# Attention phases: the norm moved to the step before the projections, and the row maxima transposed, split and sent in two halves of the heads

## The chip, the cores and the metric

The kernel runs on one core of one Trainium2 chip. The metric is the device time of one execution in microseconds (us), the median of several executions. All durations below come from one profiled execution of the kernel before.

## What is computed

A four-layer transformer with adaptive layer norm over x of shape 16 x 256 x 128. Four of its parts are softmax attentions and are touched here; they carry the tile prefixes a0, a1, a2 and a4. For each batch row (256 tokens of 128 features) each of them computes

```python
h = _layernorm(x, axis=-1) * (1 + ca) + sa          # a4: RMS norm with a gain
q, k, v = project(h)                                # a4: rotary position on q and k
scores = jnp.einsum('bhqd,bhkd->bhqk', q, k) / scale
scores = jnp.where(jnp.asarray(causal), scores, -jnp.inf)   # a2: no mask
attn = jax.nn.softmax(scores, axis=-1)
out = jnp.einsum('bhqk,bhkd->bhqd', attn, v)
x = x + ga * (out @ w_out)
```

The head size is 8. a0, a2 and a4 have 16 query heads, a1 has 32 (pairs of them are subtracted from each other with a weight, and the result gets a root-mean-square norm of its own). The expert and feed-forward parts (f0 to f4), the linear attention and the norms between the parts are not touched.

## The kernel before

`attention_phase` runs one attention for all 16 batch rows. Its five engine programs walk through **steps** t = -2 to 16, and each step has one **slot** per head, 16 or 32 of them (`NH`). In step t the stages of different batch rows overlap: row t+2 is normed and projected, row t+1 gets its scores for the maxima, row t gets transposed scores, exponentials and the product with V, and row t-1 is finished. The slot at which an engine issues a piece is a constant (`L_QK`, `L_SPLIT`, `L_NMQ` and so on); each engine runs its pieces in the order of the slots and waits in that order, since an instruction never overtakes another one of its engine. `U` is 1 for 16 heads and 2 for 32.

The stages of one batch row, with the lines of the profile:

- **Norm.** L606 mean (matmul into bank 6), L755 XC, L481 square, L611 variance, L759 VE, L438 power -0.5 on POOL, L763/764 diagonal DG, L617 broadcast, L768 XN, L487 H. Slots 0 to 5 (times U).
- **Projections.** L628/629 (a4: L625/626) compute q and k from H into bank 6 at slot 6 (a4: q at 6, k at 8), DVE copies them to QKF one slot later, L634 computes v at slot 12 (22 for a1).
- **Split.** q and k are kept as three bf16 parts. L498 casts the high part (slot 8, in a4 slot 10), L448 on POOL takes the rest, L501 casts the middle part one slot later, L451 on POOL makes the low part. SP then issues 14 DMAs of 64 KB (a1: 26; L417/419), which lay the parts out by head in QH and KH, after two small ones that zero two rows (L413). The semaphore is `parts_sent`.
- **Scores for the maxima.** From slot 2 of the next step, two heads a slot (`score_slots`), L549 to L551 (a2: L554/555) write bank 0 or 1 and the reduce at L742 (a2: L745) takes their maxima. The first waits for `parts_sent`.
- **Maxima.** At slot 10 (`L_NMQ`, a1: 23), when all heads are reduced, L805/806 gather the maxima in NMQ, L688 transposes them into bank 7, L506 casts the high half (slot 11), L809 takes the low half, and ACT itself issues two small DMAs (L510, slot 12) that put both into rows of QH. The semaphore is `m_sent`.
- **Transposed scores.** In the next step, one head a slot, L567 to L569 (a2: L572/573), with the maxima already in the product; the first waits for `m_sent` of all heads. ACT exponentiates (L525), PE multiplies with V in bursts every fourth slot (L590), ACT copies a set (L471), PE turns it (L597, bank 7), DVE divides (L722, L728 or L733/735).
- **Output.** L670 transposes the context into bank 7 at slot 6, L519 copies it, L675 multiplies with the output weights, L829 (a4: L827) makes TMP at slot 8 and L832 adds it to x. In a1 there is a norm before it: L515, L815, a power on POOL (L455), L821.

Bank 7 is shared by the turns, the transposed maxima and the output, so each of them waits until the one before it has been read.

```python
L_MEAN, L_VAR, L_POW, L_DG, L_BC, L_XN, L_QK, L_V = 0, 2, 2, 3 * U, 4 * U, 5 * U, 6 * U, 10 * U + 2
L_SPLIT = [10] if rope else [L_QK + 2 + 2 * r * U for r in range(R)]
L_NMQ = L_SCORES + N_SCORES
...
after(pe, p_ready, b, p - 1)
if p == 0:
    after(pe, m_sent, b)
```

## Time and profile before

| | |
|---|---|
| median of 3 runs | 5114.13 us (5106.98 to 5117.71) |
| profiled execution, its own time | 5110.65 us |
| its span | 5108.9 us |
| mean granted TensorE clock | 0.804 of 2.4 GHz |
| TensorE matmul busy | 3976.6 us (78%) |
| VectorE busy | 2662.7 us (52%) |
| ScalarE busy | 1604.8 us (31%) |

Engines are PE (TensorE), DVE (VectorE), ACT (ScalarE), POOL (GpSimd) and SP (SyncE, which only issues DMAs here). In the rows a matmul reads `bank<-stationary,moving`. A row's bracket gives the idle time of its engine just before it and what ended that. The granted clock has two levels, 1.2 and 2.4 GHz, and a mean of 0.804 lies between them.

### The profile page before, as it was taken

The numbers are of one execution on the slowest core, as the hardware profiler recorded it, in microseconds if no ns is written. First come the engines' busy times: TensorE is split into PE (matmuls) and PEld (weight loads), VectorE is DVE, ScalarE is ACT, GpSimd is POOL, SyncE is SP. The second block draws the span as 40 slices with busy tenths as digits, with TensorE's granted clock in tenths as the row PEclk, the third lists the DMA queues.
The fourth block names the chain that finished last, engine by engine and source line by source line (L and its number), as shares of the span: only waits on it lengthen the run. The fifth ranks groups of instructions, "written<-read, shape, count | busy, mean of one in ns | idle before, by whom it ended". The sixth has DMA issues, their size and how long they took to land. (4 is left out here: it accounts for less than half of the span.)

```text
span 5108.9 us, 74218 instructions
## 1 busy us (share of the span) xinstructions
PE 3976.6 (78%) x20856; PEld 2273.6 (45%) x20936; DVE 2662.7 (52%) x5663; ACT 1604.8 (31%) x3308; POOL 592.7 (12%) x462
## 2 busy tenths in 40 slices
PE   4776679999957676767999789856666899546799
PEld 3454634444435454545444344434444545213544
DVE  4444655454466555644333355553333556896455
ACT  1434132222224444443333244423333322112321
POOL 1110100000012122210000011111111101442100
PEclk6878589999968888887999867776666798556699
DMA  3222100000032323220000000002222000000000
GB/s 57 32 28 26 50 9 1 1 0 0 4 42 29 38 28 40 28 51 3 1 1 0 6 19 18 18 13 26 25 26 37 3 0 0 2 0 5 20 1 16
DMA packets 150267, 89.53 MB, mean 18 GB/s; under 512 B 19049, under 2 KB 147315, under 8 KB 149235
## 3 DMA queue, kind: packets, MB, share of 16 engines
q1 hardware_dynamic: 143666, 81.61, 11.6%
q10 hardware_dynamic: 5760, 2.93, 0.3%
q0 software_dynamic: 576, 1.80, 0.2%
q8 instruction: 125, 2.05, 0.2%
q14 instruction: 140, 1.14, 0.1%
HBM read 26.35 MB, written 2.10 MB: 6 GB/s over the span
## 5 line engine op out<-in xcount | busy, mean ns | idle before, releaser
L525 ACT ACTIVATE a1PR<-bank 128x384 f32<-128x384 f32 x512 | 248.6, 492 | 302.2 <-PE bank L569 299.1
L1346 DVE TENSOR_TENSOR f1eHS<-f1eSG,bank 128x512 f32<-128x512 f32 x256 | 175.9, 687 | 319.8 <-PE bank L1274 229.8
L1341 DVE TENSOR_TENSOR f0eT<-f0eSG,bank 128x512 f32<-128x512 f32 x256 | 175.9, 687 | 312.7 <-PE bank L1255 293.2
L1305 ACT ACTIVATE f0eSG<-bank 128x512 f32<-128x512 f32 x256 | 152.8, 597 | 557.3 <-PE bank L1252 557.3
L1252 PE MATMUL bank<-f1NT,f1W 128*128 (+1 forms) x576 | 297.0, 597 | 15.0 <-DMA f1eSELB<-in_sel 14.8
L742 DVE TENSOR_REDUCE a1NM<-bank 128x3 f32<-128x384 f32 x512 | 266.1, 552 | 62.2 <-PE bank L551 56.2
L1274 PE MATMUL bank<-f1eHS,f1W 128*128 128x512 f32 x576 | 293.8, 592 | 1.2
L1252 PE MATMUL bank<-f0NT,f0W 128*128 (+1 forms) x512 | 262.5, 594 | 17.1 <-DMA f0eSELB<-in_sel 17.1
L1305 ACT ACTIVATE f1eSG<-bank,f1eFB 128x512 f32<-128x512 f32 x256 | 175.9, 687 | 283.6 <-PE bank L1252 152.8
L1274 PE MATMUL bank<-f0eHS,f0W 128*128 128x512 f32 x512 | 261.3, 592 | 1.6
L1255 PE MATMUL bank<-f0NT,f0W 128*128 (+1 forms) x512 | 262.3, 594 | 0.0
L742 DVE TENSOR_REDUCE a4NM<-bank 128x3 f32<-128x384 f32 x256 | 130.2, 550 | 164.6 <-PE bank L551 164.0
L525 ACT ACTIVATE a4PR<-bank 128x384 f32<-128x384 f32 x256 | 121.6, 489 | 267.7 <-PE bank L569 266.8
L1346 DVE TENSOR_TENSOR f0eHS<-f0eT,bank 128x512 f32<-128x512 f32 x256 | 175.9, 687 | 54.6 <-PE bank L1274 49.7
L745 DVE TENSOR_REDUCE a2NMQ<-bank 128x2 f32<-128x512 f32 x256 | 162.6, 682 | 68.4 <-PE bank L555 66.8
L525 ACT ACTIVATE a2PR<-bank 128x512 f32<-128x512 f32 x256 | 146.5, 594 | 140.2 <-PE bank L573 140.0
L549 PE MATMUL bank<-a1KH,a1QH 128*128 128x128 bf16 x512 | 126.5, 249 | 71.4 <-DVE a1NM L742 65.7
L525 ACT ACTIVATE a0PR<-bank 128x384 f32<-128x384 f32 x256 | 121.1, 490 | 191.2 <-PE bank L569 171.3
L1252 PEld LDWEIGHTS bank<-f1NT,f1W 128*128 128x128 f32 x576 | 109.3, 191 | 155.9 <-issue 154.3
L567 PE MATMUL bank<-a1QH,a1KH 128*128 128x128 bf16 x512 | 122.0, 241 | 70.8 <-DMA a1QH<-a1M 63.6
L742 DVE TENSOR_REDUCE a0NM<-bank 128x3 f32<-128x384 f32 x256 | 130.1, 551 | 85.8 <-PE bank L551 84.8
L1274 PEld LDWEIGHTS bank<-f1eHS,f1W 128*128 128x128 f32 x576 | 109.4, 190 | 130.1 <-issue 120.0
(597 smaller groups left out, 9286.8 us busy)
## 6 DMA issues: line engine op xcount, KB each, us to landing
a1QH<-a1SPL SPq DMA_DIRECT2D x192, 64.0 KB
a1KH<-a1SPL SPq DMA_DIRECT2D x192, 64.0 KB
a0QH<-a0SPL SPq DMA_DIRECT2D x96, 64.0 KB
a0KH<-a0SPL SPq DMA_DIRECT2D x96, 64.0 KB
f0W<-in_w SPq DMA_DIRECT2D x3, 2048.0 KB, 13.4
a2QH<-a2SPL SPq DMA_DIRECT2D x96, 64.0 KB
a4QH<-a4SPL SPq DMA_DIRECT2D x96, 64.0 KB
a4KH<-a4SPL SPq DMA_DIRECT2D x96, 64.0 KB
```

What stands on the lines that cost most here:

```text
L525: nc.scalar.activation(PR[:, h % 8, :], bank[2 + h % 2][:, 0:NC], ACT.Exp, scale=SCALE)\
L549: pe.matmul(o[:, 0:P], q(0), k(0), start=True, stop=True)
L567: pe.matmul(o[:, 0:P], k(0), q(0), start=True, stop=True)
L742: v.tensor_reduce(NM3[:, h, :], bank[h % 2][:, 0:NC].rearrange("p (n k) -> p n k", n=3), AX, ALU.max, negate=True).then_inc(s_used.sem, 1)
L745: v.tensor_reduce(NMQ[:, :, h], bank[h % 2][:, 0:NC].rearrange("p (n k) -> p n k", n=2), AX, ALU.max, negate=True).then_inc(s_used.sem, 1)
L1252: pe.matmul(bank[q][:, :], W1[:, m * P:(m + 1) * P], x, start=True, stop=True).then_inc(g_ready.sem, 1)
L1255: pe.matmul(bank[2 + q][:, :], W3[:, m * P:(m + 1) * P], x, start=True, stop=True).then_inc(u_ready.sem, 1)
L1274: mm = pe.matmul(bank[6 + j][:, :], W2[:, m, :], HS[:, m % 4, :], start=(m == 0), stop=(m == NCH - 1 and CBF is None))
L1305: nc.scalar.activation(dst, bank[q][:, :], fn, bias=FB[:, m:m + 1] if cfg.get("hbias") else 0.0)\
L1341: v.tensor_tensor(T1[:, :], a, bank[2 + q][:, :], ALU.mult).then_inc(t1_ready.sem, 1)
L1346: v.tensor_tensor(HS[:, m % 4, :], a, bank[4 + (j * NBC + kth[m]) % 2][:, :], ALU.mult).then_inc(hs_ready.sem, 1)
```

## The change

In every attention phase the norm of a batch row runs one step earlier than its projections (stage t+3, with H in three buffers), so the steps begin at t = -3, and the slots are dealt out anew. Projections come at slot 0 (a1: 0 and 4; a4: 0 and 2), the high cast at slot 2 (a1: 2 and 6; a4: 5), the middle cast two slots after it, v at slot 2 (a1: 8; a4: 4), and the norm takes the slots behind v. The maxima go in two halves of the heads, each with a transpose, a cast, a subtraction and two DMAs of its own, at slots 7 and 10 (a1: 13 and 24), on semaphores `m_sent_0` and `m_sent_1`; the transposed scores wait for the second half at head NH/2. The turns come one slot earlier, and with them the output.

The diff, cut to its core (U, R, QK as above; HG is NH/2):

```diff
         SPL = sb("SPL", [P, R, 3, 2, T], BF16)
         NM3 = sb("NM3", [P, NH, 3])
...
+        M2 = sb("M2", [HG, 2, 2, T], BF16)
         ZR = sb("ZR", [NH, T], BF16)
...
-                for k in range(2, 5):
+                for k in range(1, 4):
                     step(i * 3 + k, k % 3)
-            for t in range(14, 17):
+            for t in range(13, 17):
                 step(t, t % 3)
...
-        L_MEAN, L_VAR, L_POW, L_DG, L_BC, L_XN, L_QK, L_V = 0, 2, 2, 3 * U, 4 * U, 5 * U, 6 * U, 10 * U + 2
-        L_SPLIT = [10] if rope else [L_QK + 2 + 2 * r * U for r in range(R)]
+        L_QK = [2 * n * U for n in range(QK)]
+        L_V = 2 * QK * U if not rope else 4
+        L_SPLIT = [5] if rope else [L_QK[r] + 2 for r in range(R)]
+        L_MEAN = L_V + 2
+        L_SQ = L_MEAN + 2 if centered else L_MEAN
+        L_VAR = L_SQ + U
+        L_VE = L_VAR + 1
+        L_DG = L_VE + U
+        L_BC = L_DG + 1
+        L_XN = L_BC + 1
+        L_H = L_XN + 1
         L_SCORES = 2
         N_SCORES = cfg["score_slots"]
         heads_at = lambda h: range(*(min(max(k - L_SCORES, 0), N_SCORES) * NH // N_SCORES for k in (h, h + 1)))
-        L_NMQ = L_SCORES + N_SCORES
-        L_MT = L_NMQ
-        L_MSPLIT = L_MT + 1
-        L_MSEND = L_MSPLIT + 1
+
+        L_NMQ = [13, 24] if diff else [7, L_SCORES + N_SCORES]
         burst_at = lambda h: ((h - 5) // 4 % NU, 0 if h >= 5 else -1) if h % 4 == 1 else None
         copy_at = {(4 * PK * (s + 1) + 2) % NH: (s, (4 * PK * (s + 1) + 2) // NH) for s in range(NS)}
-        turn_at = {4 * PK * (s + 1) + 4: s for s in range(NS)}
+        turn_at = {4 * PK * (s + 1) + 3: s for s in range(NS)}
...
+        turned_at = {p + 1: s for p, s in turn_at.items()}
         late = lambda h, at: [(s, p // NH) for p, s in at.items() if p % NH == h]
-        L_LAST = 4 * PK * NS + 4 - NH
+        turns_before = lambda h: sum(p < h for p in turn_at)
+        L_LAST = 4 * PK * NS + 3 - NH
         L_COMBINE = L_LAST + 2
         L_CTT = L_COMBINE + 4 if diff else L_LAST + 2
         L_OUT, L_TMP = L_CTT + 1, L_CTT + (1 if diff else 2)
...
-                        b = t + 2
-                        if h == L_POW:
+                    if has(3, t):
+                        b = t + 3
+                        if h == L_VE:
                             after(pool, ve_ready, b)
                             after(pool, dg_ready, b - 1)
                             nc.gpsimd.tensor_tensor(RS[:, :], VE[:, :], c.HALF[:, 0:2], ALU.pow).then_inc(rs_ready.sem, 1)
+                    if has(2, t):
...
-                        if h == L_MEAN:
+                    if has(3, t):
+                        b = t + 3
+                        if h == L_SQ:
...
-                        if h == L_XN:
+                        if h == L_H:
                             after(act, xn_ready, b)
-                            after(act, v_ready, b - 1)
+                            after(act, v_ready, b - 3)
                             scale, shift = (c.MOD[:, l, 1, one(b)], c.MOD[:, l, 0, one(b)]) if centered else (COL[:, 3:4], 0.0)
-                            nc.scalar.activation(H[:, :], XN[:, :], ACT.Identity, bias=shift, scale=scale).then_inc(h_ready.sem, 1)
+                            nc.scalar.activation(H[:, m, :], XN[:, :], ACT.Identity, bias=shift, scale=scale).then_inc(h_ready.sem, 1)
+                    if has(2, t):
+                        b = t + 2
...
@@ -496,18 +511,20 @@
                                 after(act, f_ready, b, None if rope else r + 1)
                                 after(act, parts_sent[r], b - 1)
                                 nc.scalar.copy(SPL[:, r, 0, :, :], QKF[:, :, :]).then_inc(hi_ready.sem, 1)
-                            if h == L_SPLIT[r] + 1:
+                            if h == L_SPLIT[r] + 2:
                                 after(act, res_ready, b, r + 1)
                                 nc.scalar.copy(SPL[:, r, 1, :, :], RES[:, :, :]).then_inc(mid_ready.sem, 1)
-                    if has(1, t) and h == L_MSPLIT:
+                    for g in range(2 if has(1, t) else 0):
                         b = t + 1
-                        after(act, mt_ready, b)
-                        after(act, m_sent, b - 1)
-                        nc.scalar.copy(M2[:, 0, :], bank[7][0:NH, 0:T]).then_inc(mhi_ready.sem, 1)
-                    if has(1, t) and h == L_MSEND:
-                        after(act, mlo_ready, t + 1)
-                        for a in range(2):
-                            act.dma_start(QH[MAX0 + a:MAX0 + a + 1, (m + 1) % 3, :, :], M2[:, a, :]).then_inc(m_sent.sem, 16)
+                        if h == L_NMQ[g] + 1:
+                            after(act, mt_ready, b, g + 1)
+                            after(act, m_sent[g], b - 1)
+                            nc.scalar.copy(M2[:, g, 0, :], bank[7][0:HG, 0:T]).then_inc(mhi_ready.sem, 1)
+                        if h == L_NMQ[g] + 2:
+                            after(act, mlo_ready, b, g + 1)
+                            for a in range(2):
+                                act.dma_start(QH[MAX0 + a:MAX0 + a + 1, (m + 1) % 3, g * HG:(g + 1) * HG, :], M2[:, g, a, :])\
+                                    .then_inc(m_sent[g].sem, 16)
                     if has(-1, t):
                         b = t - 1
                         if diff and h == L_COMBINE:
...
 
             def scores_t(b, j, p):
                 after(pe, p_ready, b, p - 1)
-                if p == 0:
...
             def step(t, m):
                 for h in range(NH):
                     if has(2, t):
-                        b = t + 2
+                        b, j = t + 2, (m + 2) % 3
...
+                                if rope:
+                                    w = (WQ, WK)[n]
+                                    pe.matmul(bank[6][:, 0:T], w[:, 0:P], H[:, j, :], start=True, stop=True)
+                                    mm = pe.matmul(bank[6][:, T:2 * T], w[:, P:2 * P], H[:, j, :], start=True, stop=True)
+                                else:
+                                    pe.matmul(bank[6][:, 0:T], WQ[:, n * P:(n + 1) * P], H[:, j, :], start=True, stop=True)
+                                    mm = pe.matmul(bank[6][0:KR, T:2 * T], WK[:, n * P:n * P + KR], H[:, j, :], start=True, stop=True)
+                                mm.then_inc(qk_ready.sem, 1)
+                        if h == L_V:
+                            after(pe, qk_copied, b)
+                            for n in range(2):
+                                mm = pe.matmul(bank[6][:, n * SV * VW:(n + 1) * SV * VW], H[:, j, n * P:(n + 1) * P], WV[:, :],
+                                               start=True, stop=True)
+                            mm.then_inc(v_ready.sem, 1)
+                    if has(3, t):
+                        b = t + 3
                         if h == L_MEAN and centered:
                             after(pe, v_copied, b - 1)
...
@@ -645,15 +664,12 @@
                     for s, back in late(h, turn_at):
                         if has(-back, t):
                             b = t - back
-                            if s == 0 and not diff:
+                            after(pe, cx_ready, b, s)
+                            if turns_before(L_OUT) == s and not back:
                                 after(pe, tmp_ready, b - 1)
-                            else:
-                                after(pe, cx_ready, b, s)
-                            if s == (1 if diff else 0):
-                                after(pe, tmp_ready, b - 1)
-                            if 4 * PK * (s + 1) + 4 - 4 * PK < L_MT < 4 * PK * (s + 1) + 4 and has(1 - back, t):
-                                after(pe, mhi_ready, b + 1)
-                                after(pe, mlo_ready, b + 1)
+                            for g in range(2):
+                                if turns_before(L_NMQ[g]) == s and not back and has(1, t):
+                                    after(pe, mlo_ready, t + 1, g + 1)
                             turn(b, s)
                     if has(-1, t):
                         b = t - 1
...
                             mm.then_inc(o_ready.sem, 1)
-                    if has(1, t) and h == L_MT:
+                    for g in range(2 if has(1, t) else 0):
                         b = t + 1
-                        if causal:
-                            after(pe, nmq_ready, b)
-                        else:
-                            after(pe, s_used, b)
-                        if diff and has(0, t):
-                            after(pe, cx_ready, t, (L_MT - 8) // 4 + 1)
-                        if has(-1, t):
-                            after(pe, tmp_ready, t - 1)
-                        for n in range(2):
-                            mm = pe.transpose(bank[7][0:NH, n * P:(n + 1) * P], NMQ[:, n, :], c.ID)
-                        mm.then_inc(mt_ready.sem, 1)
+                        if h == L_NMQ[g]:
+                            if causal:
+                                after(pe, nmq_ready, b, 2 * g + 2)
+                            else:
+                                after(pe, s_used, b, HG * (g + 1))
+                            if has(0, t):
+                                after(pe, cx_ready, t, turns_before(L_NMQ[g]))
+                            if has(-1, t):
+                                after(pe, tmp_ready, t - 1)
+                            if g:
...
                             maxima(b, n)
-                        if h == L_NMQ and causal:
-                            after(v, s_used, b)
-                            v.tensor_copy(NMQ[:, 0, :], NM3[:, :, 0]).then_inc(nmq_ready.sem, 1)
-                            v.tensor_tensor(NMQ[:, 1, :], NM3[:, :, 1], NM3[:, :, 2], ALU.min).then_inc(nmq_ready.sem, 1)
-                        if h == L_MSPLIT:
-                            after(v, mhi_ready, b)
-                            v.tensor_tensor(M2[:, 1, :], bank[7][0:NH, 0:T], M2[:, 0, :], ALU.subtract).then_inc(mlo_ready.sem, 1)
+                        for g in range(2):
+                            heads = slice(g * HG, (g + 1) * HG)
+                            if h == L_NMQ[g] and causal:
+                                after(v, s_used, b, HG * (g + 1))
+                                after(v, mt_ready, b - 1, g + 1)
+                                v.tensor_copy(NMQ[:, 0, heads], NM3[:, heads, 0]).then_inc(nmq_ready.sem, 1)
+                                v.tensor_tensor(NMQ[:, 1, heads], NM3[:, heads, 1], NM3[:, heads, 2], ALU.min).then_inc(nmq_ready.sem, 1)
+                            if h == L_NMQ[g] + 1:
+                                after(v, mhi_ready, b, g + 1)
+                                v.tensor_tensor(M2[:, g, 1, :], bank[7][0:HG, 0:T], M2[:, g, 0, :], ALU.subtract).then_inc(mlo_ready.sem, 1)
```

In `maxima`, and for the turns on DVE, only waits are changed to fit; the operations are the same.

The order on ACT in a4, in the loop over steps, of before. a4SPL<-a4QKF is the high cast, a4SPL<-a4RES the middle cast, a4M the halves of the maxima, a4CTS a set's copy, a4PR an exponential:

```order
L498 CAST a4SPL<-a4QKF 128x512 [waits parts_sent]
...
L525 ACTIVATE a4PR<-bank 128x384 [waits st_ready]
...
L471 COPY a4CTS<-bank 128x256 [waits t_ready]
...
L501 CAST a4SPL<-a4RES 128x512 [waits res_ready]
...
L506 CAST a4M<-bank 16x256 [waits m_sent]
...
L510 DMA a4QH<-a4M 1x16x256 [waits mlo_ready]
```

The same engine and phase after the change, from the high cast to the first pair of DMAs (a4CTT is the copy ahead of the output product):

```order
L513 CAST a4SPL<-a4QKF 128x512 [waits parts_sent]
...
L536 ACTIVATE a4CTT<-bank 128x256 [waits o_ready]
L236 ISA
L542 ACTIVATE a4PR<-bank 128x384 [waits st_ready]
...
L516 CAST a4SPL<-a4RES 128x512 [waits res_ready]
...
L522 CAST a4M<-bank 8x256 [waits m_sent_0]
...
L526 DMA a4QH<-a4M 1x8x256 [waits mlo_ready]
...
L522 CAST a4M<-bank 8x256 [waits m_sent_1]
...
L526 DMA a4QH<-a4M 1x8x256 [waits mlo_ready]
```

The two casts of the split stood between the exponentials just ahead of the maxima's cast; now they stand well ahead of both halves, and there are two casts of maxima and four DMAs where there were one and two.

The order on PE in a4 after the change, at slot 7, where the first half of the maxima is transposed (L707) between the last transposed scores of slot 7 (L584 to L586) and the next scores for maxima (L566); before, no transpose stood among the scores for maxima:

```order
L584 MATMUL bank<-a4QH,a4KH 128x128 [waits p_ready]
L585 MATMUL bank<-a4QH,a4KH 128x128
L586 MATMUL bank<-a4QH,a4KH 128x128
L236 ISA
L236 ISA [waits nmq_ready]
L236 ISA [waits cx_ready]
L707 MATMUL bank<-CST,a4NMQ 8x128 [waits tmp_ready]
L707 MATMUL bank<-CST,a4NMQ 8x128
L236 ISA
L566 MATMUL bank<-a4KH,a4QH 128x128 [waits s_used]
```

The transpose waits for the gathered maxima of half the heads and for TMP of the row before, and the scores behind it wait with it.

## Rows read from the trace of the kernel before

**Rows 1.** Windows of eleven steps in a0, a1, a2, a4: stretch, length, busy us, PEclk.
```profile
143.34:443.95 300.61, 213.45 (x2068) 148.60 (x2068) 136.05 (x352) 118.52 (x276) 33.05 (x33) 0.80 0.29 30
1573.58:2146.03 572.45, 395.91 (x4048) 284.63 (x4048) 327.88 (x891) 244.51 (x550) 118.16 (x66) 0.83 0.30 34
3004.77:3285.71 280.94, 254.37 (x1726) 132.52 (x1728) 157.48 (x341) 132.45 (x264) 35.25 (x33) 0.76 0.08 18
3511.18:3875.06 363.88, 228.37 (x2090) 162.75 (x2090) 137.61 (x363) 116.81 (x276) 49.06 (x55) 0.67 0.25 25
```
**Rows 2.** Waits in a4's window: us in total, times, longest.
```profile
PE bank L549 <- DMA a4QH<-a4SPL: 68.1, 11, 7.7
PE bank L567 <- DMA a4QH<-a4M: 23.5, 11, 2.5
PE bank L597 <- DVE a4M L809: 19.5, 11, 1.9
ACT a4SPL L498 <- POOL a4QKF L442: 17.0, 11, 1.5
PE bank L688 <- DVE a4NMQ L806: 15.8, 11, 1.4
```
**Rows 3.** Waits in a0's window.
```profile
PE bank L567 <- DMA a0QH<-a0M: 36.6, 11, 4.3
PE bank L549 <- DMA a0QH<-a0SPL: 18.9, 11, 3.1
```
**Rows 4.** Waits in a1's window.
```profile
PE bank L567 <- DMA a1QH<-a1M: 42.0, 9, 6.8
PE bank L670 <- DVE a1CX L733: 40.8, 11, 3.7
```
**Rows 5.** Waits in a2's window.
```profile
PEld bank L572 <- DMA a2QH<-a2M: 4.0, 7, 1.0
PE bank L554 <- DMA a2QH<-a2SPL: 3.3, 3, 1.2
```
**Rows 6.** Timeline of a4: start us, us, engine line op out<-in, [idle before <-releaser].
```profile
3638.05 1.21 SPq L413 DMA_DIRECT2D a4QH<-a4ZR  x2
...
3640.74 1.17 ACTq L510 DMA_DIRECT2D a4QH<-a4M  x2
...
3646.04 0.29 PE L567 MATMUL bank<-a4QH,a4KH 128*128 128x128 bf16 x1 [2.30 <-DMA a4QH<-a4M]
...
3646.79 1.51 PE L590 MATMUL bank<-a4PR,a4VX 128*32 128x256 f32 x16
...
3655.13 0.29 PE L549 MATMUL bank<-a4KH,a4QH 128*128 128x128 bf16 x1 [5.89 <-DMA a4QH<-a4SPL]
```
**Rows 7.** Timeline of a0 around the maxima of one step.
```profile
326.36 0.54 DVE L829 TENSOR_SCALAR a0TMP<-bank,a0COL,MOD 128x256 f32<-128x256 f32 x1
...
326.95 0.86 PE L590 MATMUL bank<-a0PR,a0VX 128*32 128x256 f32 x16
...
327.53 1.01 DVE L742 TENSOR_REDUCE a0NM<-bank 128x3 f32<-128x384 f32 x2
...
328.98 0.38 PE L688 MATMUL bank<-CST,a0NMQ 128*16 128x128 f32 x2 [0.89 <-DVE a0NMQ L806]
...
329.88 0.41 DVE L809 TENSOR_TENSOR a0M<-bank,a0M 16x256 bf16<-16x256 f32 x1 [1.04 <-ACT a0M L506]
...
330.33 1.39 ACTq L510 DMA_DIRECT2D a0QH<-a0M  x2
...
338.24 0.29 PE L567 MATMUL bank<-a0QH,a0KH 128*128 128x128 bf16 x1 [4.17 <-DMA a0QH<-a0M]
```
**Rows 8.** Timeline of a1: the value projection, and the power on POOL.
```profile
1771.09 1.13 PE L634 MATMUL bank<-a1WV,a1H 128*128 128x256 f32 x4
...
1797.03 5.43 POOL L455 TENSOR_TENSOR a1CR<-a1CM,HALF 128x32 f32<-128x32 f32 x1 [5.92 <-DVE a1CM L817]
```

More of the change, by code:

```diff
@@ L738, in maxima @@
                 after(v, s_ready, b, h + 1)
-                if h == 0:
+                if h == 0 and not causal:
                     after(v, mt_ready, b - 1)
@@ L832, in step @@
                             v.tensor_tensor(DST[:, tok(b)], DST[:, tok(b)], TMP[:, :], ALU.add).then_inc(x_updated.sem, 1)
[L833 removed]
+                    for s, back in late(h, turned_at):
                         if has(-back, t):
                             turned(t - back, (m - back) % 3, s)
[L836 to L837 removed]
+                if isinstance(t, int) and t < -1:
+                    fill(t + 4)
             steps(v, step)
```

101 lines of the change are left out of this document (45 added, 56 removed).

## The prediction

> **What bounds the kernel now.** I read the granted clock first: it is 0.804 on average, so part of the matmul time is run at 1.2 GHz. Then the busy time by stretches, to find the touched phases, and in each a window of eleven steps, cut from one square of the norm to the eleventh after it [rows 1]. The columns there are the stretch, its length, then the busy time of PE, PE's weight loads, DVE, ACT and POOL, then the granted clock. Divided by 11, one step takes 27.3 us in a0, 52.0 in a1, 25.5 in a2 and 33.1 in a4. PE is busy 19.4, 36.0, 23.1 and 20.8 us of them, at a clock of 0.80, 0.83, 0.76 and 0.67. DVE has 12.4, 29.8, 14.3 and 12.5 us of work, ACT 10.8, 22.2, 12.0 and 10.6. So no engine but PE in a2 is near its limit. a0 and a4 do nearly the same arithmetic, and a4 takes 5.8 us more: there a wait must stand.
>
> Next the waits in the four windows. In a4 [rows 2] PE waits for the parts of q and k (a4SPL) 68.1/11 = 6.2 us a step and for the maxima (a4M) 23.5/11 = 2.1. In a0 [rows 3] it is 1.7 and 3.3, in a1 [rows 4] 42.0/11 = 3.8 for the maxima, in a2 [rows 5] 0.3 and 0.4. These are waits of the engine that all the others follow, so they lie on the path.
>
> The timeline shows why. In a4 SP issues its first DMA behind the high cast at 3638.05 and the scores that need the last of them start at 3655.13 [rows 6]: 17.1 us from cast to landing. The two small DMAs of the maxima are issued at 3640.74, and the first transposed scores start at 3646.04, 5.3 us later; in a0 it is 330.33 to 338.24, 7.9 us [rows 7]. After the high cast a4 has six slots left in the step and two in the next, which are worth 17.1 less the two waits of 6.2 and 2.1, some 9 us; after the issue of the maxima every phase with 16 heads has four slots left. Both are less than the landing takes.
>
> **What the change does to each wait.** The high cast moves from slot 8 to slot 2 in a0, from 10 to 5 in a4, so its DMAs have 16 and 13 slots before the scores need them. If a step is some 22 us long, the cast in a4 comes about 6 us into it (estimate: 22/16 us a slot, less a little, since the first slots have no scores) and lands at 6 + 0.6 + 17.1 = 24; the scores at slot 2 want it at 22 + 3 = 25 (same estimate). So the parts' wait goes, in a4 with about 1 us to spare. The first half of the maxima goes out at slot 9 instead of 12, some 10 to 11 us into the step, plus 5.3 to 7.9 for landing: 16 to 19, ahead of the next step at 22. The second half still goes at slot 12, but is wanted only at head 8. In a1 the halves have 17 and 22 slots. That wait goes everywhere.
>
> Per step, waits removed: a0 1.7 + 3.3 = 5.0, a1 3.8, a2 0.7, a4 6.2 + 2.1 = 8.3.
>
> **The clock.** After the wait in a4 a burst with V takes 1.51 us for 16 matmuls [rows 6], in a0 at the upper level 0.86 [rows 7], so a wait costs again in what follows it. At full clock PE's busy time would shrink by 19.4 x 0.20 = 3.9 us in a0, 36.0 x 0.17 = 6.1 in a1, 20.8 x 0.33 = 6.9 in a4, and 23.1 x 0.24 = 5.5 in a2. From both sides: nothing of it is a gain (the clock stays as it is), or most of it. The nearest row is a2: it hardly waits for a DMA, and is at 0.76. So full clock is not what follows when those waits are gone. I take a quarter: 1.0, 1.5 and 1.7 us, and nothing in a2.
> The Trainium skill (TensorE: Matmul & The Clock Gate, "Loop structure matters more than you think") says that a DMA wait between groups of matmuls drops the clock and that matmuls kept back to back hold it. By that rule alone the whole reduction would be had, which is the first rival; the rows of a4 agree with the first half of it, the clock of a2 speaks against the second.
>
> **Other gains.** In a4 the casts of the split stand right ahead of the maxima's cast in ACT's order, and the high cast waits 17.0/11 = 1.5 us for POOL. PE then waits 1.4 us for the gathered maxima (L688) and 1.8 us at the turn for their low half (L597) [rows 2]. The new order has both casts out of the way; in a0, where they always were, L688 waits 0.89 [rows 7]. I take 1.8 of the 3.2 us. In a1 PE waits 40.8/11 = 3.7 us for the context [rows 4], behind a power of 5.43 us on POOL [rows 8]. The power stays, but the projection of v, 1.13 us [rows 8], now stands at slot 8 in front of that wait instead of at slot 22: 0.6 us gained. POOL now has part of the split around the power, and ACT's middle cast of the second half may have to wait for it at slot 8; that is in the 1.1 below.
>
> **New costs.** A second pair of transposes (0.38 us), a second cast and subtraction (0.41), and a second pair of DMAs on ACT's queue, which holds ACT for 1.39 us [rows 7]. ACT's share and the subtraction lie in the slots in which DVE sets the pace with its two reduces of 1.01 us together, and ACT has half its time free: nothing, while DVE stays slower there. The norm's pieces on DVE leave those slots in about the same number as new ones enter. What counts is the place on PE: at slot 7 the first transposes wait for the gathered maxima and for TMP (0.54 us [rows 7]), and the scores behind them wait too, so DVE runs dry for some 0.3 us (estimate: transposes 0.38 plus the first scores, less the addition to x that DVE still has). The turn now follows the second half's transposes after one slot instead of two; between them lies the chain of 1.04 us wait and 0.41 us subtraction: 0.2 more. Sum 0.9 us a step in a0 and a4. In a2, where PE is busy 91% of the time, I put 1.2, in a1 1.1. Bounds of this cost: 0 (all of it beside DVE's reduces) and 5.6 (last rival).
> The Trainium skill (DMA: Bandwidth & Descriptors, "Rules for kernel authors") speaks against this part: small transfers should be coalesced, since under 64 KB one pays mostly overhead. The halves are 4 KB each. The rows show that overhead as 1.39 us of ACT's queue a pair; if all of it were exposed, the sum would be worse by 1.39 x 64 = 89 us.
>
> The added step t = -3 holds one norm, which stood at the start of step -2 before: nothing.
>
> **The sum**, per batch row: a0 -5.0 - 1.0 + 0.9 = -5.1; a1 -3.8 - 1.5 - 0.6 + 1.1 = -4.8; a2 -0.7 + 1.2 = +0.5; a4 -8.3 - 1.7 - 1.8 + 0.9 = -10.9. Together -20.3, times 16 batch rows = -325 us. The profiled execution took 5110.65 us, so 4786; the median of the runs is 3.5 us above it, so **4789 us**.
>
> **Rivals.**
> 1. *The clock stays up too.* Half of the shrinking in a0, a1 and a4 and 4 us in a2, where PE is nearly the limit: 1.0 + 1.5 + 1.7 + 4.0 = 8.2 us a row beyond my sum, 131 us: 4658. For it: the low stretches follow waits in a0 and a4. Against: a2. Chance 0.13.
> 2. *Only the waits go, and new ones take part of it.* No clock gain, none of the 1.8 and 0.6, and twice the new costs: a0 -3.2, a1 -1.6, a2 +1.7, a4 -6.5, together -9.6 x 16 = -154: 4960. For it: PE, DVE and ACT are in lockstep in every slot. Chance 0.13.
> 3. *The DMAs become the floor of a4.* The step there can't be shorter than 17.1 + 0.6 plus the way from slot 2 to slot 5, three pairs of reduces and the rope work, 3 to 4 us: 21 to 22. If the four small DMAs in the same traffic stretch the landing by 2 us, the step is 24 instead of 22.2: +29 us, 4818. Chance 0.12.
> 4. *Slower: PE's order.* The transposes now stand among the scores, and nothing overtakes them. Each first half could stop PE for two reduces, TMP, transposes and subtraction (1.01 + 0.54 + 0.38 + 0.41 = 2.3), each second for the gathering and the chain to the turn (0.89 + 1.04 = 1.9), and ACT's issue be exposed (1.39): 5.6 us in each of 64 steps, 358 us against 285 us of removed waits (17.8 x 16): +73, 5187. It decides from 4.5 us a step on. Against: in before the same chain costs PE about 1 us a step in a0. Chance 0.04.
> 5. *No effect:* another engine holds the step at its length. DVE's 12.4 of 27.3 us speaks against it, and the order shows that casts and sends do move. Chance 0.03.
>
> **How the numbers follow.** The forecast has 0.55. The range 4690 to 4920 holds it with its bounds, rival 3 and part of rivals 1 and 2; outside lie about half of each of these two, the slower case and no effect. A measurement of this kernel tells 0.2%, 10 us, from no change. Faster by more: 0.55 + 0.13 + 0.13 + 0.12 = 0.93; within: 0.03; slower: 0.04.
>
> **What would show it.** In the changed profile the step of a4 should be 21 to 24 us, a0 21 to 23, a1 46 to 49, a2 25 to 27. PE's waits for the maxima should be near 0 in all phases and for the parts near 0 in a0, under 1 us in a4. New waits should show at the first half's transposes, ended by DVE, of 1 to 2 us on PE. I am wrong if a4's wait for parts is still over 2 us, if a2 loses over 2 us a step, or if the transposes' waits sum to over 4 us a step.

## The result, and the profile after

The changed kernel takes **4894.3 us** (median of 4, 4886.36 to 4904.15) against 5115.92 (4 runs, 5106.98 to 5130.74) of the kernel before: ratio 0.9565, 95% interval 0.9535 to 0.9595. The forecast was 4789 in a range of 4690 to 4920: the direction and the range held, but only two thirds of the expected gain came. The number lies nearer to rival 2 (4960, new waits eat part of the gain) than to the forecast.

| | before | after |
|---|---|---|
| span of the profiled execution, us | 5108.9 | 4902.4 |
| mean granted clock | 0.804 | 0.827 |
| TensorE matmul busy, us | 3976.6 | 3986.4 |
| a0, first memset to last TMP, us | 484.7 | 403.5 |
| a1 | 880.4 | 885.0 |
| a2 | 452.1 | 459.7 |
| a4 | 563.2 | 416.6 |

The four phases sum to -215.6 us; the rest of the kernel, which the change does not touch, took 9 us more in this profile. The windows of after that answer to [rows 1], again from one square of the norm to the eleventh after it (stretch, length, busy time of PE, its weight loads, DVE, ACT, POOL, then clock), in the order a0, a1, a2, a4:

```profile
120.21:365.29 245.08, 202.36 (x2091) 139.88 (x2091) 142.68 (x386) 118.76 (x287) 33.07 (x33) 0.85 0.35 37
1473.28:2040.45 567.17, 416.12 (x4070) 286.24 (x4070) 339.47 (x925) 245.13 (x562) 117.80 (x66) 0.81 0.32 34
2910.33:3191.43 281.10, 234.63 (x1739) 125.26 (x1738) 163.09 (x354) 134.45 (x276) 33.05 (x33) 0.84 0.07 17
3415.78:3666.27 250.49, 204.27 (x2113) 139.21 (x2113) 144.68 (x397) 116.58 (x288) 49.18 (x55) 0.89 0.35 36
```

Divided by 11, a step and its split into PE busy and PE idle:

| phase | before: step = busy + idle | after | predicted step |
|---|---|---|---|
| a0 | 27.3 = 19.4 + 7.9 | 22.3 = 18.4 + 3.9 | 22.2 |
| a1 | 52.0 = 36.0 + 16.0 | 51.6 = 37.8 + 13.7 | 47.2 |
| a2 | 25.5 = 23.1 + 2.4 | 25.6 = 21.3 + 4.2 | 26.0 |
| a4 | 33.1 = 20.8 + 12.3 | 22.8 = 18.6 + 4.2 | 22.2 |

The step is as forecast within 0.6 us in three phases; a1 alone is off, by 4.4, and outside the 46 to 49 us that the prediction named for it. Now the waits of PE in the same windows. In a4, where [rows 2] had 68.1 and 23.5 us of DMA waits:

```profile
PE bank L707 <- DVE a4TMP L851: 15.5, 11, 1.4
PE bank L614 <- DVE a4M L833: 11.2, 11, 1.2
...
PE bank L584 <- DMA a4QH<-a4M: 3.6, 4, 2.6
```

The wait for the parts is gone, that for the maxima is 0.3 us a step. The new wait stands at the first half's transposes (L707), 1.4 us a step and ended by DVE, where the prediction looked for it. a0 has the same pair (15.1 and 11.3 us) and no DMA wait. In a1 the 42.0 us of [rows 4] for the maxima are gone too, but:

```profile
PE bank L566 <- DVE a1NM L761: 45.8, 89, 1.0
PE bank L686 <- DVE a1CX L752: 40.4, 11, 4.6
PE bank L614 <- ACT a1CTS L484: 30.1, 33, 2.2
PE bank L707 <- DVE a1CX L752: 10.9, 11, 1.1
PE bank L630 <- issue: 10.4, 3, 3.5
```

and ACT stands once a step at the middle cast of a1's second half, because POOL does its 5.43 us power first. This is the timeline of one such place (start, duration, engine and line, idle time before it and what ended that):

```profile
1770.09 5.43 POOL L468 TENSOR_TENSOR a1CR<-a1CM,HALF 128x32 f32<-128x32 f32 x1 [3.21 <-DVE a1CM L841]
...
1775.48 1.15 POOL L461 TENSOR_TENSOR a1RES<-a1QKF,a1SPL 128x512 f32<-128x512 f32 x1
1775.55 1.63 DVE L845 TENSOR_TENSOR a1CX<-a1CX,a1CR 128x512 f32<-128x512 f32 x1 [2.55 <-POOL a1CR L468]
1776.66 0.62 ACT L516 CAST a1SPL<-a1RES 128x512 bf16<-128x512 f32 x1 [5.05 <-POOL a1RES L461]
```

Two suspects come from this: ACT blocked for 5.05 us, and DVE's scaling of the context, which starts with POOL's subtraction and takes 1.63 us.

The end of a phase gained nothing either. These are the two steps in which the phase a2 runs empty, first of before, then of after; they do the same attention work, in nearly the same number of matmuls (142 and 108, then 140 and 117):

```profile
3302.90:3325.10 22.20, 19.65 (x142) 9.89 (x142) 12.35 (x25) 10.90 (x22) 1.45 (x2) 0.77 0.09 21
3325.10:3338.60 13.50, 11.21 (x108) 5.04 (x108) 3.70 (x10) 9.02 (x19) 0.00 (x0) 1.00 0.01 2
```
```profile
3221.40:3249.40 28.00, 25.21 (x140) 11.74 (x140) 12.80 (x26) 10.72 (x22) 0.00 (x0) 0.54 0.00 1
3249.40:3271.90 22.50, 19.74 (x117) 8.55 (x118) 5.28 (x13) 9.73 (x20) 0.00 (x0) 0.54 0.01 2
```

At 0.54 PE is busy for 19.7 us in the second of them, and was for 11.2 at full clock.

### The profile page after: what moved, and what is told of

Same layout as the page of the kernel before. It is cut to its first block and busy times, and to the rows that moved or that the text cites. A ratio compares the mean times of both kernels' runs of the same rounds, so it can differ in the third digit from the quotient of the medians.

```text
span 4902.4 us, 75514 instructions
## 1 busy us (share of the span) xinstructions
PE 3986.4 (81%) x21064; PEld 2255.4 (46%) x21064; DVE 2695.0 (55%) x5823; ACT 1612.1 (33%) x3372; POOL 584.9 (12%) x462
## 3 DMA queue, kind: packets, MB, share of 16 engines
q1 hardware_dynamic: 143666, 81.61, 12.2%
## 5 line engine op out<-in xcount | busy, mean ns | idle before, releaser
L1370 DVE TENSOR_TENSOR f0eHS<-f0eT,bank 128x512 f32<-128x512 f32 x256 | 176.0, 688 | 54.6 <-PE bank L1298 49.6
L566 PE MATMUL bank<-a1KH,a1QH 128*128 128x128 bf16 x512 | 127.0, 248 | 74.6 <-DVE a1NM L761 66.4
L1276 PEld LDWEIGHTS bank<-f0NT,f0W 128*128 128x128 f32 x512 | 97.7, 191 | 139.6 <-issue 139.2
## 6 DMA issues: line engine op xcount, KB each, us to landing
f0W<-in_w SPq DMA_DIRECT2D x3, 2048.0 KB, 12.2
```

The source lines that it names most:

```text
L566: pe.matmul(o[:, 0:P], q(0), k(0), start=True, stop=True)
L1276: pe.matmul(bank[q][:, :], W1[:, m * P:(m + 1) * P], x, start=True, stop=True).then_inc(g_ready.sem, 1)
L1370: v.tensor_tensor(HS[:, m % 4, :], a, bank[4 + (j * NBC + kth[m]) % 2][:, :], ALU.mult).then_inc(hs_ready.sem, 1)
```

## The experiments

The table gives what all comparisons below rest on: the window from the fourth to the fifteenth square of each phase, divided by 11, as PE busy + PE idle at the mean granted clock. It is one profiled execution each; the ratios are against the kernel before in the same session. How far a step can be read shows where kernels have the same code in a phase: after, e1, e2 and e5b agree within 0.6 us in a0 and 0.2 in a4, e10 and e13 within 0.1 in a1, but in a2 e9b, e10 and e13 have 24.7, 24.7 and 22.5. A difference of 2 us in a2 shows nothing by itself.

| kernel | us, ratio | a0 | a1 | a2 | a4 |
|---|---|---|---|---|---|
| before | 5115.9 | 19.4+7.9 .80 | 35.9+16.0 .83 | 23.7+2.3 .74 | 20.6+12.2 .68 |
| after | 4894.3, .9565 | 18.1+3.9 .87 | 37.8+13.7 .81 | 21.9+4.0 .82 | 18.5+4.2 .90 |
| e1 | 4816.9, .9398 | 17.7+4.1 .89 | 33.2+13.2 .92 | 21.7+4.0 .83 | 18.5+4.4 .90 |
| e2 | 4806.6, .9388 | 17.7+4.0 .90 | 34.2+11.7 .87 | 21.9+4.0 .81 | 18.4+4.4 .90 |
| e3 | 4920.5, .9589 | 18.0+4.0 .87 | 38.4+13.4 .77 | 23.0+3.6 .77 | 19.5+6.0 .85 |
| e4 | 5195.6, 1.0128 | 20.3+8.1 .76 | 36.6+12.9 .83 | 25.0+4.3 .71 | 20.5+13.3 .73 |
| e5b | 4864.2, .949 | 17.4+4.1 .91 | 37.3+13.0 .82 | 22.9+3.7 .78 | 19.0+3.7 .86 |
| e6b | 4860.1, .9458 | 17.6+4.0 .89 | 35.5+11.1 .84 | 23.2+3.6 .76 | 19.9+6.0 .83 |
| e8b | 5183.3, 1.0111 | 21.0+7.6 .74 | 35.8+14.7 .84 | 25.6+4.0 .68 | 20.0+11.3 .74 |
| e9b | 4790.7, .9316 | 16.2+3.5 .97 | 34.6+11.7 .85 | 22.6+2.0 .76 | 18.4+7.1 .87 |
| e12 | 4875.5, .9512 | 16.9+4.0 .93 | 34.9+12.7 .86 | 28.4+1.8 .57 | 19.2+4.5 .84 |
| e10 | 4712.9, .922 | 15.9+3.2 .98 | 33.6+10.4 .87 | 22.7+2.1 .76 | 18.6+5.0 .87 |
| e13 | 4683.3, .9192 | 16.1+3.2 .97 | 33.3+10.5 .88 | 20.1+2.5 .88 | 19.0+3.7 .86 |
| e14 | 4838.2, .9433 | 16.5+3.2 .95 | 39.4+13.6 .75 | 21.6+2.4 .83 | 19.0+3.9 .86 |

**e1: the second projection of a1 moved away from the power.**

```diff
-        L_QK = [2 * n * U for n in range(QK)]
-        L_V = 2 * QK * U if not rope else 4
+        L_QK = [0, 8] if diff else [2 * n * U for n in range(QK)]
+        L_V = 12 if diff else 2 * QK * U if not rope else 4
```

> Only in a1: the second projection goes from slot 4 to 8, its split from slot 6 to 10, v from 8 to 12, and the norm follows. The power on POOL then stands ahead of the second split in time. Theory A (POOL's order: the second split waits behind the power of 5.4 us, ACT's middle cast waits 4.9 us for it, and POOL's subtraction next to DVE's scaling of the context stretches that): both waits go, a step of a1 falls from 51.6 to about 47.5 us, the kernel by some 60 us to 4835. Theory B (the turns, one slot earlier, cost it: PE waits 2.7 us a step for ACT's copies): nothing changes, 4894.

Measured 4816.93 us (4812.91 to 4818.9), 77 under the changed kernel, and a1's step is 46.4 instead of 51.5. ACT's wait for POOL fell from 54.6 to 0.7 us in eleven steps. Theory A's number holds, with a little more than it gave, so the loss does hang on the slots that a1's second half was given. But the two windows say how: idle time is nearly equal (13.7 and 13.2 us a step), PE busy is not (after first, then e1):

```profile
1424.50:1990.50 566.00, 415.82 (x4070) 286.09 (x4068) 338.82 (x924) 245.10 (x563) 117.79 (x66) 0.81 0.33 35
```
```profile
1419.60:1930.10 510.50, 364.82 (x4072) 255.03 (x4070) 324.70 (x926) 240.70 (x563) 118.38 (x66) 0.92 0.35 38
```

The same 4070 matmuls take 51 us less, at 0.92 instead of 0.81. Of 5.0 us a step, 4.6 are the clock.

**e2: e1, and a1's turns and what follows them back in their old slots.**

```diff
-        turn_at = {4 * PK * (s + 1) + 3: s for s in range(NS)}
+        turn_at = {4 * PK * (s + 1) + (4 if diff else 3): s for s in range(NS)}
-        L_LAST = 4 * PK * NS + 3 - NH
+        L_LAST = 4 * PK * NS + (4 if diff else 3) - NH
```

(and a1's second maxima at slot 23 instead of 24.)

> The same as the first kernel, and in a1 also the turns one slot later, as they were before the change, with the second half of the maxima at slot 23. Theory A: within 10 us of the first kernel. Theory B: PE's waits for ACT's copies fall from 2.7 to under 1 us a step, a1 gains 1.7 to 2.7 us a step, 25 to 40 us in all.

4806.55 us (4803.01 to 4818.29): 10 us under e1, less than the two spreads can tell apart, as theory A has it. In the profile a1 has 1.5 us a step less idle time and 1.0 more busy time.

**e3: maxima in one piece, the rest of the change kept.** `L_NMQ` is `[24]` in a1 and `[10]` elsewhere, one transpose, cast, subtraction and pair of DMAs for all heads.

> The changed kernel with the maxima in one piece again (slot 10, in a1 24), the norm ahead kept: half of the change alone. If the halves are what removes the waits for the maxima, these come back (3.3, 3.8, 0.4 and 2.1 us a step in a0, a1, a2, a4, together 9.6) and the halves' own cost goes (about 1 us in each): 5.6 x 15 = 84 us more than the changed kernel, 4978. If the earlier split alone clears the DMA traffic for them, they stay near 0 and it is about 60 us faster than the changed kernel, 4835.

4920.52 us (4899.98 to 4933.78): the median is 26 us over the changed kernel's, 12% of its gain, in between the two theories. The intervals of the two ratios overlap, but the profiles put the difference in a4, where the step is 25.4 instead of 22.7. What the halves were for, the wait for the maxima, is gone in a0 without them. The DMA issues show why. In a0 ACT sends the maxima long after SP's last part and well before its next one:

```profile
271.77 0.61 SPq L429 DMA_DIRECT2D a0QH<-a0SPL  x1
...
279.29 1.15 ACTq L527 DMA_DIRECT2D a0QH<-a0M  x2
...
285.89 1.21 SPq L425 DMA_DIRECT2D a0QH<-a0ZR  x2
```

In before, the maxima of a0 were issued in the middle of SP's twelve parts, and their reader started 7.9 us later [rows 7]. (The DMAs of 64 KB are twelve a batch row, and 24 in a1; the 14 and 26 named with the stages include the two small ones.) In a4 of e3 they still go out right behind the parts in some steps, and 2.7 us behind them in others:

```profile
3523.44 0.61 SPq L429 DMA_DIRECT2D a4QH<-a4SPL  x1
...
3524.41 1.15 ACTq L527 DMA_DIRECT2D a4QH<-a4M  x2
...
3532.63 0.29 PE L585 MATMUL bank<-a4QH,a4KH 128*128 128x128 bf16 x1 [4.57 <-DMA a4QH<-a4M]
...
3550.15 0.61 SPq L429 DMA_DIRECT2D a4QH<-a4SPL  x1
...
3552.83 1.15 ACTq L527 DMA_DIRECT2D a4QH<-a4M  x2
...
3559.26 0.23 PE L585 MATMUL bank<-a4QH,a4KH 128*128 128x128 bf16 x1 [1.62 <-DMA a4QH<-a4M]
```

From issue to the first reader it is 8.2 us in the first case and 6.4 in the second, and PE's wait falls from 4.57 to 1.62. Over a whole phase the median from issue to landing of the maxima's DMAs is 3.2 us in before and 1.9 in e3 for a0, 4.2 and 2.1 for a1. So moving the norm ahead also takes the parts' traffic out of the way of the maxima.

**e4: halves and earlier turns alone, with norm, projections and casts in their old slots and step.**

```diff
+        L_QK = [6 * U + 2 * n * U for n in range(QK)]
+        L_V = 10 * U + 2
+        L_SPLIT = [10] if rope else [L_QK[r] + 2 for r in range(R)]
+        L_MEAN, L_SQ, L_VAR, L_VE, L_DG, L_BC, L_XN, L_H = 0, 0, 2, 2, 3 * U, 4 * U, 5 * U, 5 * U
```

> The maxima in two halves and the turns one slot earlier as in the changed kernel, but norm, projections and casts in the slots and the step where they were before: the other half of the change alone. If the two parts each remove their own wait: the parts' wait stays (1.7 us in a0, 6.2 in a4), the maxima's goes, 9.6 - 4 = 5.6 us a row, 84 us less than before, 5030. If the halves only pass the wait on to the parts: a4 gains nothing and the kernel is within 20 us of 5115 less what a0 and a1 give, some 5070.

5195.57 us (5177.36 to 5208.45), 1.3% slower than before (interval 0.9% to 1.7%), where both theories had it faster. No wait for the maxima is left, in any phase, and yet a4's step is 33.8 instead of 32.8. PE's waits in a4 are now (compare [rows 2]):

```profile
PE bank L559 <- DMA a4QH<-a4SPL: 78.9, 11, 8.3
PE bank L607 <- DVE a4M L826: 26.1, 11, 2.4
PE bank L700 <- DVE a4TMP L844: 17.1, 11, 1.6
PE bank L700 <- DVE a4NMQ L823: 11.5, 11, 1.2
```

The two DMA waits of before, 68.1 + 23.5 = 91.6 us, have become one of 78.9: the wait for the maxima stood just ahead of the wait for the parts, and what it gives back is mostly waited for two slots later. The rest went to the turns (L607, 19.5 before) and to TMP (L700). In a0 it is 36.6 + 18.9 = 55.5 before [rows 3] and 45.6 in e4.

**e5b: after, with a1's second middle cast at slot 11 and no other change.** This takes ACT's wait away and leaves POOL's order and its overlap with DVE.

```diff
-                            if h == L_SPLIT[r] + 2:
+                            if h == L_SPLIT[r] + (5 if diff and r else 2):
```

> The changed kernel with one number different: in the two-softmax phase (a1) the middle cast of the second half stands at slot 11 instead of 8. GpSimd still does the normalization's power (5.43 us) ahead of its share of that split, beside VectorE. Theory A1 (the cost was ScalarE standing in order behind a cast whose input was late, 4.9 us a step): the 54 us of wait of ScalarE in eleven steps go, a1's step falls from 51.5 to about 46.5 us as in e1, and the time comes to 4815 to 4850 us. Rival A2 (the cost is VectorE and GpSimd stretching each other in that stretch, whatever ScalarE does): the step stays at 50 or more, 4880 to 4900 us.

4864.22 us (4857.83 to 4890.06), between both. ACT's wait went from 54.6 to 0.6 us, and a1's step from 51.5 only to 50.3: theory A1 falls as an account of the 5 us, since it gives 1.1. A2 fits this step, and DVE's scaling, 1629 ns in after (and 1628 in e5b), takes 693 ns in e1, which seems to speak for it:

```profile
L845 DVE TENSOR_TENSOR a1CX<-a1CX,a1CR x11: 1629/1629/1631, 1463.5 to 1981.1; 128x512 f32<-128x512 f32 x11
```
```profile
L845 DVE TENSOR_TENSOR a1CX<-a1CX,a1CR x11: 693/693/694, 1452.0 to 1915.4; 128x512 f32<-128x512 f32 x11
```

But it is 1629 ns again in e2, whose a1 step is 45.9 us, beside 46.4 in e1, and in e13, the fastest kernel of all, with 43.8 us. So A2 falls too: the stretch by 0.94 us is real and costs little.

**e6b: e1 with one piece everywhere.**

> e1 with the maxima in one piece in all four phases. Theory (halves pay only where the maxima's transfer is still waited for, which e3's trace has as 2.6 us a step in a4 and nothing elsewhere): a4's step 25.4 instead of 22.9, thirteen times, so 4816.9 + 20 to 40 = 4837 to 4857 us. Rival 1 (with a1's step 5 us shorter, its transfer of the maxima is waited for again, up to the 3.8 us a step that it cost before the change): another 50, about 4900. Rival 2 (no piece matters, e3's difference was the clock): 4815 to 4820.

4860.09 us (4845.21 to 4870.17), 43 over e1, just above the end of what the theory gave and far from rival 1. a4 is 25.9 (+3.0 us), a2 26.9 (+1.2), a1 46.6 (+0.1): in a1 no wait for the maxima came back. The halves pay in a4; the 1.2 us of a2 are within what equal code differs by there.

**e8b: before with the turns one slot earlier, nothing else.** e4's slots with `NP = 1`, so one piece; a1's maxima come at slot 24 instead of 23.

> The kernel before with one thing of the change alone: the transposes of the context stand one slot earlier, and what follows them with them; maxima in one piece, normalization in its old place. e4 (this and the halves) measured 1.4 % over before. Theory T (the cost is in the earlier transposes, which wait for VectorE's update of X to leave their bank, 1.7 us a step in e4's a0 and a2): nearly all of e4's loss shows here, 5170 to 5200 us. Theory H (the cost is in the second set of casts, transposes and sends): 5110 to 5135 us, as before.

5183.26 us (5169.42 to 5204.26), ratio 1.0111 (1.0069 to 1.0154): most of e4's loss, theory T by the number. The wait that T named, for the update of X, is not there. In a0 PE waits for DVE's reduces instead, a wait that before's list for these steps does not have:

```profile
PE bank L560 <- DVE a0NM L755: 24.8, 25, 1.6
```

In a0 and a2 the step rises by 1.3 and 3.6 us, and PE's busy time by 1.6 and 1.9 at a lower clock (.80 to .74 and .74 to .68); a1 and a4 are 1.4 and 1.5 us shorter, which does not make up for it.

**e9b: the norm ahead alone.** e3 with the turns back: one piece, turns in their old slots (`turn_at` + 4, `L_LAST` with them, a1's maxima at slot 23).

> The changed kernel with the normalization one step ahead and nothing else: maxima in one piece, the transposes of the context in their old slots (e3 had them one slot earlier, 4920.5 us). Theory T (the earlier transposes cost 1.5 to 3 us a step wherever they stand): 50 to 100 us under e3, 4820 to 4870. Theory H or none: 4910 to 4925, as e3. e1 and e2 differ by the turns of a1 alone and are equal within 10 us, which speaks for the latter at least in a1.

4790.68 us (4762.93 to 4806.57), 130 us under e3 and 104 under the full change; more than theory T had given. a0 of e3, then of e9b:

```profile
95.30:336.90 241.60, 197.71 (x2088) 135.25 (x2081) 138.68 (x353) 114.91 (x277) 33.07 (x33) 0.87 0.36 38
```
```profile
96.90:313.50 216.60, 178.12 (x2072) 122.20 (x2068) 135.27 (x349) 116.86 (x276) 33.04 (x33) 0.97 0.42 42
```

and two of PE's waits there, e3 and e9b:

```profile
PE bank L567 <- DVE a0NM L762: 21.9, 41, 1.5
PE bank L615 <- DVE a0M L834: 11.6, 11, 1.2
```
```profile
PE bank L615 <- DVE a0M L834: 8.0, 11, 0.8
...
PE bank L567 <- DVE a0NM L762: 4.8, 20, 0.3
```

With the turn one slot earlier PE waits 21.9 instead of 4.8 us in eleven steps for DVE's reduces of the scores (as I read it, DVE has the turned context to scale just then). Idle time changed by about 0.5 us a step in sum, the busy time by 1.8 at .87 and .97: the greater part is again the clock. The ends of the phases went back too: the two steps in which a2 runs empty are 25.0 and 13.5 us here, where after has 28.0 and 22.5.

**e12: the full change with the turns back**, halves transposed at slots 8 and 10 (13 and 23 in a1).

> The changed kernel with the transposes of the context (and what follows them) back in their old slots; normalization ahead and halves stay, their sends at slots 8 and 10 (13 and 23 in a1). With e3 and e9 (one piece, turns early and back: 4920.5 and 4790.7) and the changed kernel (4894.3) this fills a square of four. Theory T (the early turns cost about 2.3 us a step in a0, 5.4 in a1, 1.9 in a2, half of it and more as a lower clock of TensorE): steps of 19.7, 46.3 and 24.7 as in e9, and in a4, where e9 still waits 4.3 us a step for the maxima, 21 to 23; 4740 to 4790 us. Rival H (the halves' second set of casts and sends crowds the slots just as the early turns do): 4800 to 4880.

4875.52 us, but with a spread that needs a look: 4879.98, 4873.87, 4877.18 and 4814.17, with clocks of .815, .816, .817 and .833. The median lies in the range of rival H, but H's reason, crowded slots, covers little of it: over e9b a0 and a1 have 1.2 and 1.3 us a step more, and a4 has 1.9 less. Against the changed kernel a0 and a1 came down, to 20.9 and 47.6 us a step from 22.0 and 51.5. Of the 87 us by which the four phases of e12 are over those of e9b in the profiles, 84 are a2, which went up to 30.1 with hardly any wait left:

```profile
2802.70:3134.30 331.60, 312.10 (x1742) 162.37 (x1738) 162.97 (x349) 135.24 (x276) 33.00 (x33) 0.57 0.06 16
```

In a1, e9b and e12 show where the loss came from. With the turns in their old slots POOL's power stands at slot 6, behind the second split, and with the early turns at slot 5, ahead of it. This is POOL in e12, where after has the power first:

```profile
1721.22 1.15 POOL L461 TENSOR_TENSOR a1RES<-a1QKF,a1SPL 128x512 f32<-128x512 f32 x1 [1.24 <-ACT a1SPL L513]
...
1725.85 5.42 POOL L468 TENSOR_TENSOR a1CR<-a1CM,HALF 128x32 f32<-128x32 f32 x1
```

In the eleven steps ACT does not wait for POOL at its casts in either kernel, and the steps are 46.3 and 47.6 us, near the 46.4 of e1, which parts the two the other way. So the early turns and the second projection at slot 4 cost together: taking back either gives 3.9 to 5.4 us a step, and once the projection is at slot 8 the early turns cost 0.5 (e2 to e1).

**e10 and e13: the parts that pay.** Norm ahead, turns back, one piece in a0, a1, a2, halves in a4 alone, and e1's later projection in a1. e13 also gives a4 the early turns of the change, and its first half slot 7 instead of 8:

```diff
+    NP = 2 if cfg.get("plain") else 1
-        turn_at = {4 * PK * (s + 1) + 3: s for s in range(NS)}
+        turn_at = {4 * PK * (s + 1) + 5 - NP: s for s in range(NS)}
```

> Normalization ahead, turns in the old slots, one piece in a0, a1 and a2, halves in a4 alone, and a1's second projection at slot 8 as in e1. From e9: a4's step falls by up to the 4.3 us that it waits for the maxima, 35 to 50 in all; a1's step is already 46.3 there, as in e1, with no wait of ScalarE for GpSimd, so theory A (that wait was a1's whole trouble) expects nothing more: 4740 to 4760 us. Rival (the later projection brings its own 5 us a step): 4670 to 4700.

> As e10, but in a4 the turns one slot earlier with the halves, as in the changed kernel. Theory T (early turns cost wherever they stand): a4's step 1 to 2 us above e10's, 15 to 25 us in all. Rival (in a4 they pay with the halves, as the change has it): equal or 10 us below e10.

e10 4712.94 us (4692.4 to 4740.74), below theory A's 4740 and above the rival's 4700: the later projection brings 2.4 us a step in a1 (46.3 to 43.9) and not 5. e13 **4683.32 us** (4675.13 to 4724.35), ratio 0.9192 (0.9136 to 0.9249): 8.1% under before and 211 us under the change. In a4 the early turns and the earlier first half together are 0.8 us a step better, against theory T, and no wait for the maxima is left there (12.4 us in eleven steps of e10). The two intervals overlap, and the larger part of the difference between the profiles is a2 (24.7 and 22.5 us a step), where the two kernels have the same code.

**e14: e13 with the turns of a0, a1 and a2 one slot later still.**

> e13 with the turns of a0, a1 and a2, and all behind them, one slot later again (9, 17 of the next step and so on, where the kernel before has 8 and 16); a4 stays as in e13. Theory T continued (each slot gives VectorE time to have the maxima and the scaled context ready before TensorE comes to the turn; in e9 TensorE still waits 4.8 us in eleven steps for the maxima in a0 and 10.0 in a2, and 46.7 in a1 for the scaled context): steps shorter by 0.2 in a0, up to 0.5 in a2 and up to 4 in a1, 4620 to 4670 us. Rival (the old slots were the right ones: what the later turn frees at its start it takes at the end, where the output's matmuls and the halves or maxima share the bank): 4690 to 4740 us.

4838.17 us (4819.19 to 4854.58, 6 runs): 155 over e13, worse than the rival's 4740. Most of it is in a1 (53.0 us a step against 43.8), e13 first:

```profile
1385.60:1867.40 481.80, 366.41 (x4051) 260.69 (x4050) 320.35 (x892) 239.16 (x552) 117.74 (x66) 0.88 0.35 40
```
```profile
1393.10:1976.20 583.10, 433.78 (x4048) 301.95 (x4048) 326.21 (x892) 244.38 (x550) 117.66 (x66) 0.75 0.31 34
```

3.1 us a step of new waits came with 6.1 us a step of busy time at a lower clock. The old slots were the right ones for a1. Leaving them by one cost two parts clock to one part wait here and from e9b to e3; from e2 to e1, with POOL's power ahead of the second split in both, it cost 1.5 us of idle time and gave 1.0 of busy time back.

## Why the prediction was right where it was, and wrong where it was not

- **DMA waits removed: right.** Parts and maxima are no longer waited for (0.3 us a step is left in a4). PE's idle time fell by 4.0 us a step in a0 and 8.1 in a4, where the sum without its clock term has 4.1 and 9.2.
- **Clock in a0, a4, a2:** busy time fell by 1.0 in a0 (forecast 1.0) and 2.2 in a4 (1.7). In a2 idle grew by 1.8 and busy fell by 1.8, for a forecast of +0.5 together and a result of 0.0.
- **a1: the step that failed.** It was put as -3.8 -1.5 -0.6 +1.1 = -4.8 and measured -0.5. Idle fell by 2.3 instead of 3.3. This step had two terms wrong. The larger error is the clock term: forecast -1.5, measured +1.8 of busy time, at .81 after .83. I had the clock rise by a quarter wherever a DMA wait goes; in a1 new short waits stand in its place. The remark that ACT may wait for POOL named the right place (5.0 us a step of ACT), but priced it as part of 1.1 us of idle time. Moving that half of the projection away gives 5.0 us a step, 4.6 of them clock (e1); taking ACT's wait alone away gives 1.1 (e5b). What the prediction did not see is that its own earlier turns put the power ahead of that half on POOL (e12). With the end of the phase this is 81 of the 109 us by which the phases fell short of -325.
- **Times 16: too much in a4.** About thirteen steps of a phase are full; the last have no projection left and no wait to lose. a4 came to -147 instead of -174: thirteen times 10.3 us, 21 at the start, and 7 given back at the end. a0 came to -81, as forecast.
- **The earlier turns: mis-sized by a factor of ten, and covered up.** I priced them at 0.2 us a step. e3 against e9b has 2.3 in a0, 5.4 in a1 and nothing in a4 (and 1.9 in a2, too little to read there); with halves, after against e12, it is 1.1 in a0, 3.9 in a1 and 1.0 the other way in a4. That a0's -5.1 was met is luck: the norm ahead alone gives -7.6 there, more than forecast, and the rest of the change took the surplus back.
- **The halves:** forecast to remove the wait for the maxima "everywhere". The norm ahead had already done that except in a4 (e3, e6b); alone, they only pass the wait on to the parts (e4).
- **The rule against small transfers** (the Trainium skill, DMA: Bandwidth & Descriptors, "Rules for kernel authors") would, at the price in the rows, have made the halves cost up to 1.39 us a step. With the turns in their old slots they cost 1.2 us a step in a0 and 1.3 in a1 and save 1.9 in a4 (e9b to e12); with the early turns they cost nothing measurable in a0. So the rule's direction holds where the single piece already arrives in time, and not in a4; how much of the cost is the DMAs' (4 KB a half, 8 KB in a1) and how much the second transposes, cast and subtraction, no run shows.

What stays open is what sets the clock in a1. e1, e3 and e14 have the same idle time per step, 13.2 to 13.6 us, and clocks of .92, .77 and .75. It is repeatable (the runs of e1 lie within 6 us), and it does not follow the sum of the waits. That it hangs on where they stand is my reading; no run here isolates it. Matmuls that fill the wait at L686 could have told, and no run has them.

## What to carry to other kernels

Take a bundled change apart before you keep it, and measure its parts in pairs, since they do not add. The norm ahead alone gave 335 us. The early turns took 130 of them back with the maxima in one piece and 19 with halves. The halves gave 26 with the early turns and cost 85 without them, nearly all of that in a2 at the low clock; what they gave for certain was in a4. When a wait goes, ask which wait stands right behind it for the same late work, and read each window as busy plus idle time, since a schedule that moves short waits on TensorE can change its busy time by more than the waits. Count a per-step gain only over the steps that contain what is gained.

## What the runs showed of the hardware

**TensorE can stay at 1.2 GHz while it is busy nearly all the time.** Four consecutive steps of a2 in e10, same instructions in each:

```profile
2817.00:2847.90 30.90, 30.43 (x164) 16.06 (x160) 14.68 (x32) 12.03 (x26) 3.00 (x3) 0.50 0.06 15
2847.90:2878.70 30.80, 30.33 (x164) 15.97 (x157) 14.57 (x32) 11.92 (x25) 3.00 (x3) 0.50 0.06 15
2878.70:2902.40 23.70, 21.09 (x168) 11.30 (x164) 14.01 (x31) 12.02 (x26) 3.00 (x3) 0.86 0.05 11
2902.40:2923.40 21.00, 17.89 (x163) 9.73 (x156) 14.22 (x32) 12.03 (x25) 3.01 (x3) 1.00 0.09 21
```

A step is 30.8 us at 0.50 with PE busy 98% of it, or 21.0 us at 1.00 with PE busy 85%. Each kind of step is followed by its like for several steps, then the level flips with no change in the work. (Busy time is that of the profile, where the ends of matmuls are modelled.) Kernels with the same code in a2 differ in it: e9b has two such steps of 30.8 us, e13 none. In e12 eleven steps of the phase take 30.7 to 30.8 us at 0.56, up to 10 us a step more than the others. Its one run at 4814 us, with a mean clock of .833 after .815 to .817, may have spent less time there; it has no profile. The Trainium skill (TensorE: Matmul & The Clock Gate, "Part 1: The HAM clock gate") says that activity releases the throttle; these steps, at 98% busy and 1.2 GHz for three steps on end, do not agree (the last two of the three are shown). Most of these matmuls contract over 65 rows or have 32 columns of weights; whether the shape matters wasn't tried.

**DVE beside POOL.** The scaling of the context takes 691 to 694 ns or 1627 to 1631 ns and nothing between. In the fourteen profiles it is long 91 times of 224, each time beside a subtraction of POOL (in after it starts 0.07 us behind one) and never otherwise; the last three steps of a phase, which have no split, are short in every kernel. The Trainium skill (GPSIMD Engine Reference, "1. Specifications") says that GpSimd's SBUF interfaces are shared with VectorE, with contention when VectorE's instruction has two SBUF inputs; this instruction has two, and the trace agrees with a factor of 2.4. No step follows it here: e2 has the long form and e1 the short one, at 45.9 and 46.4 us.
